# Two semaphores for the stack transfers, the residual load moved behind them, and score banks that rotate by one count

## The reference

```python
h = layernorm(x)
q = Wq @ h + bq;  k = Wk @ ctx + bk;  v = Wv @ ctx + bv        # per batch, 512 x 1024
dot  = mask * (q.T @ k / sqrt(32)) - (1 - mask) * 1e6          # per head, 1024 x 1024
out  = (softmax(dot) * mask) @ v
x    = x + tanh(g_xattn) * out
x    = x + tanh(g_ffn) * fp8_matmul(layernorm(x), W2)          # 1024 x 1024
```

## Time and profile before

| | |
|---|---|
| timed executions | 2894.63 us median of 3 |
| profiled execution | 2884.45 us, span 2882.7 us |
| TensorE matmul busy | 2599.3 us, 90% |
| VectorE busy | 1994.9 us, 69% |
| GpSimd busy | 1654.8 us, 57% |
| ScalarE busy | 1431.0 us, 50% |
| DMA | 306.12 MB, mean 106 GB/s |
| mean granted TensorE clock | 0.943 |

### The profile page before, as it was taken

The page is one execution under the profiler, slowest core; times in us unless marked ns, Lnnn a source line. Parts: engine busy times, 40 slices in busy tenths (PEclk is TensorE's granted clock), DMA queues, the critical chain, the costliest instruction groups (busy, mean ns, idle before and its releaser), DMA issues.

```text
span 2882.7 us, 41018 instructions
## 1 busy us (share of the span) xinstructions
PE 2599.3 (90%) x13364; PEld 1413.9 (49%) x13425; DVE 1994.9 (69%) x3251; ACT 1431.0 (50%) x2638; POOL 1654.8 (57%) x1265
## 2 busy tenths in 40 slices
PE   5999999958999999999999999999999999888995
PEld 4888888834444444444444444444444444444442
DVE  5666667555777777777777777777777777776772
ACT  3333333314555555555555555555555555555563
POOL 2333333415666666666666666666666666666675
PEclk8999999959999999999999999999999999999998
DMA  6666666553333333333333333333343434433301
GB/s 215 244 223 229 242 235 218 190 116 69 69 76 79 77 76 77 76 76 76 76 76 76 76 78 82 76 83 83 82 83 83 83 81 84 84 79 78 76 28 38
DMA packets 208249, 306.12 MB, mean 106 GB/s; under 512 B 41240, under 2 KB 108888, under 8 KB 208064
## 3 DMA queue, kind: packets, MB, share of 16 engines
q1 hardware_dynamic: 195920, 265.80, 38.2%
q10 hardware_dynamic: 12144, 38.02, 3.7%
HBM read 200.09 MB, written 102.11 MB: 105 GB/s over the span
## 4 chain that ended last, share of the span: by engine, by line
PE 47%; DMA 19%; SPq 5%; DVE 3%; issue 3%; ACT 1%; POOL 1%; ACTq 0%; DVEq 0%; POOLq 0%
DMA q_st<-qx_scr 19%; PE o_bank L723 13%; PE s_bank L697 13%; PE x_bank L710 10%; PE d_bank L734 7%; PE x_bank L758 4%; SPq L1020 3%; DVE part_max L875 3%; ACT probs L803 1%; SPq L1016 1%; POOL pair_sum L968 1%; PE x_bank L749 1%; PE x_bank L741 1%; SPq L1017 0%; SPq L1023 0%
## 5 line engine op out<-in xcount | busy, mean ns | idle before, releaser
L968 POOL TENSOR_TENSOR pair_sum<-probs 128x512 f32<-128x512 f32 x1024 | 1283.0, 1286 | 752.0 <-ACT probs L803 752.0
L875 DVE TENSOR_REDUCE part_max<-x_bank 128x1 f32<-128x512 f32 x2048 | 1285.0, 684 | 615.0 <-PE x_bank L710 607.3
L803 ACT ACTIVATE probs<-s_bank 128x512 f32<-128x512 f32 x2048 | 1077.8, 604 | 888.1 <-PE s_bank L697 879.3
L710 PE MATMUL x_bank<-k_st,q_st 98*128 98x512 f32 x2048 | 841.7, 414 | 190.8 <-DMA q_st<-qx_scr 187.1
L697 PE MATMUL s_bank<-q_st,k_st 100*128 100x512 f32 x2048 | 886.8, 435 | 7.6 <-ACT probs L803 4.9
L697 PEld LDWEIGHTS s_bank<-q_st,k_st 100*128 100x128 f32 x2048 | 392.5, 192 | 549.0 <-issue 286.8
L723 PE MATMUL o_bank<-probs,v_t 128*32 128x512 f32 x4096 | 573.5, 633 | 0.0
L710 PEld LDWEIGHTS x_bank<-k_st,q_st 98*128 98x128 f32 x2048 | 399.8, 196 | 316.5 <-DMA q_st<-qx_scr 201.0
L734 PE MATMUL d_bank<-pair_sum,ones 128*32 128x512 f32 x2048 | 290.6, 642 | 2.4 <-POOL pair_sum L968 2.4
L322 POOL TENSOR_TENSOR stage_lo<-stage,stage_hi 128x512 fp32r<-128x512 f32 x128 | 190.0, 1509 | 120.2 <-ACT stage_hi L392 119.6
L392 ACT ACTIVATE stage_hi<-stage 128x512 fp32r<-128x512 f32 x128 | 79.8, 632 | 191.4 <-DVE stage L476 144.0
(11 more groups left out here) (99 smaller groups left out, 2097.8 us busy)
## 6 DMA issues: line engine op xcount, KB each, us to landing
k_st<-k_scr SPq DMA_DIRECT2D x96, 512.0 KB
q_st<-q_scr SPq DMA_DIRECT2D x192, 256.0 KB
c_raw<-in_ctx_dram ACTq DMA_DIRECT2D x32, 512.0 KB, 7.2
x_raw<-in_x_dram ACTq DMA_DIRECT2D x32, 512.0 KB, 6.1
k_scr<-stage_hi SPq DMA_DIRECT2D x64, 256.0 KB, 2.4
k_scr<-stage_lo SPq DMA_DIRECT2D x64, 256.0 KB, 2.6
v_scr<-stage SPq DMA_DIRECT2D x64, 256.0 KB, 2.6
q_scr<-stage_hi SPq DMA_DIRECT2D x64, 256.0 KB, 2.1
```

The source lines that it names most:

```text
L710: nc.tensor.matmul(x_bank_of("tile", k)[:, :], q_st[p][0:KX, th, h, tc * P:(tc + 1) * P], k_st[p][0:KX, h, sh * HALF:(sh + 1) * HALF], sta ...
L803: nc.scalar.activation(probs[:, c % PR, h, :], s_bank[S_BANK_OF[k]][:, :], ACT.Exp).then_inc(exp_done, 1)
L875: nc.vector.tensor_reduce(part_max[:, th, sh, at:at + 1], x_bank_of("tile", k)[:, :], AX, ALU.max).then_inc(max_done, 2)
L968: nc.gpsimd.tensor_tensor(pair_sum[:, r % 2, h], probs[:, a, h], probs[:, a + 1, h], ALU.add).then_inc(pair_done, 1)
```

## The change

The twelve stack transfers now signal two semaphores. Those that query half 0 needs (all of k, and q of half 0) come first and count on `stacked[0]`; the four of query half 1 follow and count on `stacked[1]`. TensorE waits for the first at tile i = 0 and for the second at i = 32. The residual load of quad n - 1 is issued in period n behind the stack of quad n + 1 and ahead of v, no longer at the end of period n - 1. The score banks rotate by (64 n + k) % 3, so every slot reuses the bank of three slots before, across quads too.

```diff
-            stacked = sem("stacked", at)
+            stacked = [sem(f"stacked{i}", at) for i in range(TH)]
-            STACK_DMAS = 4 + 4 * TH
+            STACK_DMAS = (8, 4)
-            S_BANK_OF = [k % NB3 for k in range(NSLOT - 1)] + [1]
-
-            def s_bank_freed(k):
-
-                return max(t for t in range(-NB3 - 2, k) if S_BANK_OF[t] == S_BANK_OF[k])
+            def s_bank_of(n, k):
+
+                return s_bank[(NSLOT * n + k) % NB3]
...
-                        if counted(NSLOT * n + s_bank_freed(k) + 1):
-                            pe.wait_ge(exp_done, NSLOT * n + s_bank_freed(k) + 1)
+                        if counted(NSLOT * n + k - NB3 + 1):
+                            pe.wait_ge(exp_done, NSLOT * n + k - NB3 + 1)
...
-                        if i == 0:
-                            pe.wait_ge(stacked, 16 * STACK_DMAS * (m + 1))
+                        if i % 32 == 0:
+                            pe.wait_ge(stacked[th], 16 * STACK_DMAS[th] * (m + 1))
...
-                        for at, part in ((0, 0), (D, 0), (2 * D, 1)):
-                            for th in range(TH):
-                                sp.dma_start(q_st[p][at:at + D, th, :, :].bitcast(F32), q_part[part][:, th]).then_inc(stacked, 16)
                         for th in range(TH):
+                            for at, part in ((0, 0), (D, 0), (2 * D, 1)):
+                                sp.dma_start(q_st[p][at:at + D, th, :, :].bitcast(F32), q_part[part][:, th]).then_inc(stacked[th], 16)
                             row = qx_q[:, bass.ds(m, 1), th * HALF:(th + 1) * HALF]
-                            sp.dma_start(q_st[p][96:98, th, :, :].bitcast(F32), row.broadcast_to((2, QH, HALF))).then_inc(stacked, 16)
+                            sp.dma_start(q_st[p][96:98, th, :, :].bitcast(F32), row.broadcast_to((2, QH, HALF))).then_inc(stacked[th], 16)
...
                         if real(n + 1):
                             stack(n + 1, 1 - p)
+                        if real(n - 1):
+                            load_res(n - 1, 1 - p)
+                        if real(n + 1):
                             load_v(n + 1, 1 - p)
...
                             spread_inv(n, 0)
-                            load_res(n, p)
```

More of the change, by code:

```diff
@@ L694, in scores @@
                             pe.wait_ge(max_set, 16 * (2 * n + th + 1))
-                        if counted(NSLOT * n + s_bank_freed(k) + 1):
-                            pe.wait_ge(exp_done, NSLOT * n + s_bank_freed(k) + 1)
-                        nc.tensor.matmul(s_bank[S_BANK_OF[k]][:, :], k_st[p][0:KS, h, j * P:(j + 1) * P],
+                        if counted(NSLOT * n + k - NB3 + 1):
+                            pe.wait_ge(exp_done, NSLOT * n + k - NB3 + 1)
+                        nc.tensor.matmul(s_bank_of(n, k)[:, :], k_st[p][0:KS, h, j * P:(j + 1) * P],
                                          q_st[p][0:KS, th, h, :], start=True, stop=True).then_inc(scores_ready, 1)
@@ L802, in exp @@
                         act.wait_ge(scores_ready, NSLOT * n + k + 1)
-                        nc.scalar.activation(probs[:, c % PR, h, :], s_bank[S_BANK_OF[k]][:, :], ACT.Exp).then_inc(exp_done, 1)
+                        nc.scalar.activation(probs[:, c % PR, h, :], s_bank_of(n, k)[:, :], ACT.Exp).then_inc(exp_done, 1)
                     def copy_o(m, th):
@@ L1015, in stack @@
                         for at, part in ((0, 0), (D, 1), (2 * D, 0)):
-                            sp.dma_start(k_st[p][at:at + D, :, :].bitcast(F32), k_part[part]).then_inc(stacked, 16)
-                        sp.dma_start(k_st[p][96:KS, :, :].bitcast(F32), kx_q[:, bass.ds(m, 1), :].broadcast_to((4, QH, S))).then_inc(stacked, 16)
-                        for at, part in ((0, 0), (D, 0), (2 * D, 1)):
-                            for th in range(TH):
-                                sp.dma_start(q_st[p][at:at + D, th, :, :].bitcast(F32), q_part[part][:, th]).then_inc(stacked, 16)
+                            sp.dma_start(k_st[p][at:at + D, :, :].bitcast(F32), k_part[part]).then_inc(stacked[0], 16)
+                        sp.dma_start(k_st[p][96:KS, :, :].bitcast(F32), kx_q[:, bass.ds(m, 1), :].broadcast_to((4, QH, S))).then_inc(stacked[0], 16)
                         for th in range(TH):
+                            for at, part in ((0, 0), (D, 0), (2 * D, 1)):
+                                sp.dma_start(q_st[p][at:at + D, th, :, :].bitcast(F32), q_part[part][:, th]).then_inc(stacked[th], 16)
                             row = qx_q[:, bass.ds(m, 1), th * HALF:(th + 1) * HALF]
-                            sp.dma_start(q_st[p][96:98, th, :, :].bitcast(F32), row.broadcast_to((2, QH, HALF))).then_inc(stacked, 16)
+                            sp.dma_start(q_st[p][96:98, th, :, :].bitcast(F32), row.broadcast_to((2, QH, HALF))).then_inc(stacked[th], 16)
                     def load_v(m, p):
```

## The result

Timed beside each other on one chip, the kernel before takes 2893.91 us (median of 4) and the changed kernel 2675.72 us (median of 4, 2664.15 to 2688.70). The ratio is 0.925, with a 95% interval of 0.9198 to 0.9302. The profiled executions differ by 2884.45 - 2675.94 = 208.5 us.

What follows compares the result with a forecast made beforehand. TensorE's wait at slot 19 for the q_st transfer was taken as the bound. Per period 7.7 - 0.1 - 2.7 - 2.2 + 0.25 = 2.95 us, times 30, plus 4.3 and 4.0: 2894.6 - 97 = 2798 us; own range 2765 to 2835.

Steps and rivals of the forecast that it cites:

- The old wait: TensorE's wait at slot 19 for the q_st transfer, with the slow clock behind it, loses 7.7 us a period.
- Half 0 in time: The first eight transfers land at t0 + 16.4, needed at 17.0; 0.1 us of wait remains at slot 19.
- The new wait: VectorE waits for den_c behind slot 23's maximum, so TensorE's maximum tile of slot 27 waits 2.7 us each period.
- VectorE's arrival: VectorE's maxima of slots 20 to 23 end, and it reaches the wait for den_c, at t0 + 22.3.
- the landing of v alone: v, behind the stack without the residual load, lands at t0 + 22.2.
- The residual adds 0.52 MB at 202 GB/s, 2.6 us: 24.8: The residual load ahead of v delays v by 2.6 us to t0 + 24.8; den_c follows at 25.0.
- The clock: TensorE's clock falls to half behind the new wait each period, costing 2.2 us; lower bound 0.
- The banks: Even score bank rotation saves 0.25 us a period at slots 60 to 63; bounds 0 and 0.35.
- The sum: Gain of 2.95 us per period, times 30: 88; 97 us together with the first two quads.
- The first one: No new wait to speak of: den_c at 23.0, stall 0.7 us, clock holds; 2670 us, chance 0.10.
- The slower case: The residual costs its 7.9 us ahead of den_c, which lands at t0 + 30.3; 2981 us, chance 0.06.
- The range: 2700 to 2860 us for the changed kernel, held at 0.79 with the second, third and fourth rival.

Runs made afterwards that it cites:

- den first: The changed kernel with the move of den_c issued ahead of the residual and v loads; 2630 us, ratio 0.9108.
- den first with the old banks: The changed kernel with the move of den_c ahead of the residual and v loads, and the old score banks; 2643 us, ratio 0.9151.
- The run without the load: The changed kernel without the residual loads from the third quad on, adding old rows instead; 2634 us, ratio 0.9121.
- 512 KB more: The changed kernel with another 512 KB load, into an unread buffer, between the residual load and v; 2740 us, ratio 0.9484.
- residual alone: The kernel before with only the residual load moved behind the stack; 2857 us, ratio 0.9898.
- 256 KB more: The changed kernel with another 256 KB load, into an unread buffer, between the residual load and v; 2730 us, ratio 0.9447.
- the order alone: The kernel before with only the six q loads grouped by query half, one semaphore kept; 2843 us, ratio 0.9849.

## Why the prediction was wrong

The mechanism was the one forecast, the sizes were not. By its steps:

**The old wait.** Right. 7.7 us a period were to go; before less den first, without the 0.25 of the banks, gives 69.59 - 61.50 - 0.25 = 7.84; den first with the old banks gives it directly, 69.59 - 61.87 = 7.72.

**Half 0 in time.** Right. Forecast at t0 + 16.4, bounds 15.8 and 17.0. In the marks of the trace the first eight transfers have landed at t0 + 15.8 in the median, and slot 19 does not wait.

**The new wait.** It exists, thirty times, at the place and with the carrier forecast. VectorE's arrival (t0 + 22.3) was right, and the landing of v alone (22.2) to 0.3. **The step that failed is "The residual adds 0.52 MB at 202 GB/s, 2.6 us: 24.8".** The run without the load shows 1.4 to 1.5, and 512 KB more cost 1.2. By its own chain (free at den_c + 1.8, wanted at t0 + 24.1) the prediction would have had 1.4 us at tile 27 with the true 23.7; it had 2.7, and 1.14 were measured. (Its 1.8 is 1.09 + 0.62 = 1.71 by its rows, 0.1 less than it took.) The bounds of this step were 23.7 and 26.5, and I took a value in the middle of them, with the full rate of 202 GB/s, although the queue's last microseconds run at 41 GB/s. Part of the difference is the order of the q loads, which the prediction put at nothing: with the old order and the residual behind the stack ("residual alone") den_c lands at 24.1, and not at 23.7. Why the rest is cheaper than its bytes stays open. It may be that the DMA engines that are done first take these bytes at no cost to the end; the runs show the prices, not the engines.

**The clock.** Forecast 2.2 us in every period, drawn from one example of 2.69 us and one of 6.21. The wait was shorter, and the clock fell in 7 of thirty periods, 1.5 us each (worked out in the last section): 0.36 us in the mean. The step failed as a consequence of the one above, but not by it alone: with 256 KB more, where tile 27 is 1.79 us late, it fell in 29 of 30, and the same single wait of 1.60 us stands in both kernels with a clock of 1.00 and of 0.53. What decides between them is open; the last section has one thing that goes with it.

**The banks.** 0.25 forecast, 0.25 measured at slot 63; a further 0.12 comes with it elsewhere (den first with old and even banks).

**The sum.** Measured per period 7.84 + 0.25 - 1.14 - 0.36 = 6.59, less 0.17 at the transposes right behind tile 27 (L746: 5.1 us over thirty periods), 6.42; the two periods differ by 69.59 - 63.15 = 6.44. Forecast 2.95. Of the 3.5 between them 1.6 are the wait, 1.8 the clock. Thirty times 3.5 is 105 of the 111 us that the profiled executions lie beyond the forecast gain of 97; 5 more came ahead of the steady part, where the first k load of the third quad starts 13.7 us earlier (693.89 to 680.21) and not 8.3. 2.8 of these 5 lie ahead of the first k load of all (582.05 to 579.21), in the part that is not touched and that ends between 578.4 and 583.4 in the traces here. The medians differ by another 10, since the kernel before ran its profiled execution 10 us below its median and the changed one on it.

**The rivals.** The first one hit the time (2670) and had the clock nearly right, with some luck: its 7.25 us a period are 0.8 above the 6.44 measured, 24 us in all, and 15 of them are made up by the 5 us ahead of the steady part and the 10 between the profiled executions and the medians. Its reason, no new wait to speak of because the end of the queue is not carried by few engines, is half true: den_c lands at 23.7, between its 23.0 and my 25.0. It was held against the rule on transfers with few members in the outermost dimension. The Trainium skill (DMA: Bandwidth & Descriptors, Rules for kernel authors) states that rule. The share of 0.21 at the end is low as it would have it, before and after, but the trace does not name the engines, the rule gives no price for bytes queued behind such an end, and moving the small transfers changed nothing (0.9992), so it should not have decided against this rival. The slower case, 7.9 us for the residual, is far off: the residual cost 1.5 behind the stack. The range missed at its lower end, although the bounds of both unknown costs reached to where they came out: with den_c at its lower bound of 23.7 and no loss of clock, the sum is 7.7 - 0.1 - 1.4 + 0.25 = 6.45 a period, 2693 in all, already outside 2700. The two are not independent, since a short wait spares the clock, and I left that corner to a rival with 0.10. The own range had a slip at its upper end as well: den_c at 25.8 with a clock loss of 3.1 gives 2849 by the same sum, not 2835.

## What to carry to other kernels

A load put in front of another in a queue costs what it moves the end of the queue, not its bytes over the rate of full flow: here, where that end is thin, it was about half, so keep the end with and without the load as two bounds. When the first wait for a queue goes, look for the next small transfer that stands behind the big ones and is wanted soon; issuing it ahead of them (den_c here) took away the new wait and 46 us. And where a wait is split by what its consumer reads first, group the loads likewise: the order alone was worth 45 us here. The even banks gained 13 us in one kernel and lost some 8 and 18 in two others, where a transfer set the period: try such a step again once the wait is gone.

## What the runs showed of the hardware

**A wait that comes in steps.** Tile 27 of the changed kernel does not start later and later as den_c does. TensorE is idle ahead of it for about 0.38 us or for about 1.60, the long one 15 times in thirty, while the reciprocal's start moves by tenths. The rows of VectorE above show why, together with GpSimd's pair adds in the same two places (the timeline again):

```profile
1397.73 4.99 POOL L965 TENSOR_TENSOR pair_sum<-probs 128x512 f32<-128x512 f32 x4 [1.98 <-ACT probs L800]
...
1459.84 4.99 POOL L965 TENSOR_TENSOR pair_sum<-probs 128x512 f32<-128x512 f32 x4 [2.00 <-ACT probs L800]
```

An add takes 4.99 / 4 = 1.25 us. In the first place the third add ends at 1397.73 + 3.74 = 1401.47; L900, with two inputs in SBUF, starts at 1401.17 and ends at 1401.53. In the second it starts at 1463.90, just after the third add has ended (1463.58), and ends at 1464.87, with the fourth (1464.83). So it is in all thirty periods: L900 takes from 0.23 to 1.35 us and ends 0.03 to 0.04 us after an add, at t0 + 24.2 or about one add later. The maxima queued behind it, and so tile 27, start in steps of one add. The Trainium skill (SBUF — State Buffer, Who interferes with whom) says that a VectorE instruction with two SBUF inputs contends with a GpSimd instruction that reads SBUF, and calls it an exclusive lock; the trace agrees, with 0.97 us against 0.36 for the same 128x16 operation. L900 takes 0.85 us in the mean here; an estimate from that: at 0.36 each time tile 27 would start 0.5 us earlier, so that of its 1.14 us the wait for den_c makes up only some 0.64. The 1.09 us that the prediction took from the reciprocal to the next maximum is one draw of such a step: here it is 0.57 in the one place and 1.18 in the other.

**A short wait can cost as much again by the clock behind it.** The changed kernel holds the comparison in itself. Against the same period of den first, where nothing waits, its periods with a short idle time at tile 27 are 0.70 us longer (15 of them), those with a long one and the clock at 1.00 are 1.90 longer (7), and those with a long one behind which the clock fell 3.40 (7; the last period is not counted). So one fall costs 1.5 us; the slow level lasts 3.4 us each time. From the changed kernel to the one with 256 KB more it is 55 us. The later start of tile 27 is 0.65 us a period, 20 us; 22 more falls at 1.5 us are 33. Another 256 KB then move den_c by 0.5 us and the time by only 10 us, since the slow clock is paid already. One thing goes with the falls: in the changed kernel the clock fell in five of the six periods with a long wait whose period before had a long one too, and in one of the eight whose period before had a short one. With 256 KB more every period has the long wait, and 29 of thirty fell. The runs do not show whether that is the cause.
